# A positive part moved to VectorE, a square to ScalarE, and one sum over four corners in place of two

## What is computed

```python
# mixer, x normalised over channels
t = einsum('bhwc,cd->bhwd', x, W).reshape(B, hw, C)
xn = xf * rsqrt(max(sum(xf * xf, -1), EPS))
sim = power(relu(einsum('bic,bjc->bij', xn, xn)), 2.0)
y = einsum('bij,bjc->bic', sim, t)
...
# deformable convolution: each of nine taps is read at a position of its own
value = (hh * hw * v1 + hh * lw * v2 + lh * hw * v3 + lh * lw * v4) * mask[..., None]
out = einsum('nhwc,cf->nhwf', value, w)
```

## Time and profile before

| | before |
|---|---|
| median of 3 runs (lowest, highest) | 4405.45 us (4403.4, 4419.57) |
| profiled execution | 4427.31 us |
| its span, first to last instruction | 4425.5 us |
| busy PE / PEld | 66% / 43% |
| busy DVE / ACT / POOL | 55% / 40% / 66% |
| mean granted TensorE clock | 0.704 |

### The profile page before, as it was taken

One profiled execution on the slowest core, in us unless ns is written; L12 is line 12 of the kernel. 1 busy time (PEld: TensorE's weight loads), 2 busy tenths in 40 slices (PEclk: granted clock), 3 DMA queues, 4 the chain that ended last, 5 costly groups with the idle time before them and its releaser, 6 DMA issues.

```text
span 4425.5 us, 51603 instructions
## 1 busy us (share of the span) xinstructions
PE 2910.2 (66%) x17810; PEld 1891.5 (43%) x17810; DVE 2435.6 (55%) x3747; ACT 1761.2 (40%) x2959; POOL 2925.6 (66%) x2608
## 2 busy tenths in 40 slices
PE   5969687586757786777777676788681357146432
PEld 2434534452446345633465345633460146135321
DVE  6354454744675456655665466655654245345775
ACT  5656466245523562355425552365231112122210
POOL 0040074777777776777767777777777777776770
PEclk8979798678856895678667886589665556555555
DMA  5000214321533132423342144313351325243446
GB/s 123 8 15 9 39 24 102 100 77 50 127 96 96 39 106 82 131 54 97 85 116 77 51 110 111 110 33 107 87 133 47 104 88 131 62 127 91 121 111 120
DMA packets 540746, 375.76 MB, mean 85 GB/s; under 512 B 465872, under 2 KB 470736, under 8 KB 540496
## 3 DMA queue, kind: packets, MB, share of 16 engines
q0 software_dynamic: 110848, 257.07, 20.1%
q1 hardware_dynamic: 429648, 115.40, 12.5%
HBM read 308.79 MB, written 89.41 MB: 90 GB/s over the span
## 4 chain that ended last, share of the span: by engine, by line
POOL 43%; PE 23%; issue 13%; DVE 11%; ACT 4%; DMA 3%; DVEq 2%; SPq 1%; ACTq 0%; POOLq 0%
POOL G L548 28%; PE PS L1689 22%; POOL shared L562 9%; POOL slot_rows L554 6%; DVE G L623 2%; DMA G<-corner_table,index 2%; DVE G L629 1%; DMA out<-experts_w 1%; DVEq L625 1%; DVE small L972 1%; DVE value L631 1%; PE PS L1724 1%; DVE st L590 1%; ACT small L1551 0%; DVE smallc L590 0%
## 5 line engine op out<-in xcount | busy, mean ns | idle before, releaser
L548 POOL DMA_INDIRECT G<-corner_table,index x1800 | 2029.3, 1127 | 681.6 <-issue 537.0
L623 DVE TENSOR_TENSOR G<-G,corner_w 128x768 f32<-128x768 f32 x600 | 541.5, 953 | 678.2 <-DMA G<-corner_table,index 678.1
L1515 ACT ACTIVATE work<-PS 128x768 f32<-128x768 f32 (+2 forms) x800 | 643.2, 822 | 541.9 <-PE PS L1689 277.8
L1689 PE MATMUL PS<-xn 128*128 128x400 f16 (+3 forms) x3200 | 647.9, 346 | 236.0 <-ACT work L1515 229.8
L951 DVE TENSOR_TENSOR work<-work 128x768 f32<-128x768 f32 (+2 forms) x496 | 479.7, 973 | 457.0 <-PE PS L1689 415.3
L554 POOL DMA_INDIRECT slot_rows<-split_a,slot x400 | 485.1, 1213 | 335.1 <-DVE slot L1046 213.5
L562 POOL DMA_INDIRECT shared<-slot_results,slot x400 | 410.1, 1025 | 349.5 <-DMA slot_results<-shared 227.8
L1689 PE MATMUL PS<-work,xm 128*64 128x400 f32 (+3 forms) x3200 | 638.0, 517 | 0.0
L1689 PEld LDWEIGHTS PS<-xn 128*128 128x128 f16 (+1 forms) x3200 | 289.8, 101 | 666.4 <-ACT work L1515 389.2
L1724 PE MATMUL PS<-ident,value 128*128 128x128 f32 x800 | 181.8, 370 | 522.3 <-DVE xq L636 275.5
L1423 ACT ACTIVATE val_cm<-PS 128x512 f32<-128x512 f32 x200 | 119.1, 596 | 694.5 <-PE PS L1724 694.3
(11 more groups left out here) (266 smaller groups left out, 3591.7 us busy)
## 6 DMA issues: line engine op xcount, KB each, us to landing
G<-corner_table,index POOLq DMA_INDIRECT x1800
corner_table<-rows_scratch SPq DMA_DIRECT2D x32, 784.0 KB
shared<-slot_rows SPq DMA_DIRECT2D x32, 512.0 KB, 7.6
slot_results<-shared SPq DMA_DIRECT2D x32, 512.0 KB
corner_table<-G SPq DMA_DIRECT2D x8, 841.0 KB, 10.5
slot_rows<-split_a,slot POOLq DMA_INDIRECT x400
shared<-slot_results,slot POOLq DMA_INDIRECT x400
experts_w<-x_scratch SPq DMA_DIRECT2D x8, 784.0 KB, 6.2
```

The source lines that it names most:

```text
L548: GP.indirect_dma_start(G[0:rows, n % 2, tap * 4 * C:(tap + 1) * 4 * C], None, tables[b % 2], bass.IndirectOffsetOnAxis(ap=index[0:rows, c ...
L623: V.tensor_tensor(g, g, bc(w, 2, C), ALU.mult)
L1515: A.activation(relu[0:rows, u % 2, :, 0:n], PS[u % 2][0:rows, :, 0:n], ACT.Relu).then_inc(s["relu_done"], 1)
L1689: return P.matmul(o, a, b, start=start, stop=stop, skip_group_check=True)
```

## The change

Five of eight steps swap engines: in steps 1, 2, 4, 5 and 7 VectorE takes the positive part straight from PSUM and ScalarE squares, so that ScalarE now squares in all eight steps and takes the positive part in 0, 3 and 6. TensorE's next similarities wait for either engine's positive part; both wait on one counter of squares, `squared`. In the weighing, the two sums become one `tensor_reduce` over the corner axis, whose input is read with channels ahead of corners; there are four pieces instead of five, and the last of them stands at step 6 of a body and waits for `val_tr`.

```diff
-MIX_SAMPLE, MIX_EVAC, MIX_ADD, MIX_WEIGH = (0, 2, 4, 6), (1, 3, 5), 7, (2, 3, 4, 6, 7)
+MIX_SAMPLE, MIX_EVAC, MIX_ADD, MIX_WEIGH = (0, 2, 4, 6), (1, 3, 5), 7, (2, 3, 4, 6)
...
                     dve.drain()
-                    if piece == 4 and b * T + t > 0:
+                    if piece == 3 and b * T + t > 0:
                         dve.wait_ge(s["val_tr"], 2 * (b * T + t))
                     if piece == 3:
-                        V.tensor_tensor(g[:, :, 0:2, :], g[:, :, 0:2, :], g[:, :, 2:4, :], ALU.add)
-                    else:
-                        V.tensor_tensor(value[:, :].rearrange("p (n c) -> p n c", n=TAPS), g[:, :, 0, :], g[:, :, 1, :],
-                                        ALU.add).then_inc(s["valued"], 1)
+                        red(value[:, :].rearrange("p (n c) -> p n c", n=TAPS), g.rearrange("p n s c -> p n c s")).then_inc(s["valued"], 1)
...
                             if u in DVE_STEPS:
-                                dve.wait_ge(s["relu_done"], g + u + 1)
-                                free = squares_taken(hn, g + u)
-                                if free > 0:
-                                    dve.wait_ge(s["mixed"], free)
-                                V.tensor_tensor(sq[0:rows, u % 4, :, 0:n], relu[0:rows, u % 2, :, 0:n], relu[0:rows, u % 2, :, 0:n],
-                                                ALU.mult).then_inc(s["sq_dve"], 1)
+                                dve.wait_ge(s["sim_done"], g + u + 1)
+                                if g + u > 1:
+                                    dve.wait_ge(s["squared"], g + u - 1)
+                                V.tensor_scalar(relu[0:rows, u % 2, :, 0:n], PS[u % 2][0:rows, :, 0:n], 0.0, None,
+                                                ALU.max).then_inc(s["relu_dve"], 1)
                             beside_mixer(k, j, u)
...
+            def square_step(s_no, half, jh, u):
+                hn, rows, n = s_no // SPH, tile_rows(jh * JB + u // 2), IWS[half]
                 if u in DVE_STEPS:
-                    act.wait_ge(s["sq_dve"], square_dve(hn, jh, u))
+                    act.wait_ge(s["relu_dve"], relus_dve(hn, jh, u))
                 else:
-                    act.wait_ge(s["sq_act"], square_act(hn, jh, u))
+                    act.wait_ge(s["relu_act"], relus_act(hn, jh, u))
+                free = squares_taken(hn, s_no)
+                if free > 0:
+                    act.wait_ge(s["mixed"], free)
+                A.activation(sq[0:rows, u % 4, :, 0:n], relu[0:rows, u % 2, :, 0:n], ACT.Square).then_inc(s["squared"], 1)
...
                         for u in range(steps(jh)):
-                            if g + u + 1 < g0 + SPH:
-
+                            if u + 1 in ACT_STEPS and u + 1 < steps(jh):
                                 if u:
-                                    squared(hn, jh, u - 1)
-                                elif jh:
-                                    squared(hn, jh - 1, SPB - 1)
+                                    act.wait_ge(s["squared"], g + u)
                                 relu_step(g + u + 1, half, jh, u + 1)
-                            if u in ACT_STEPS:
...
+                            if u == SPB - 1:
+                                act.wait_ge(s["squared"], g + u)
+                                relu_step(g + SPB, half, jh + 1, 0)
+                            square_step(g + u, half, jh, u)
                             beside_mixer(k, j, u)
...
                                 if not last:
-                                    pe.wait_ge(s["relu_done"], g + u + 1)
+                                    wait_relu(hn, jh, u)
                                     sims(half, jh * JB + (u + 2) // 2, u)
```

More of the change, by code:

```diff
@@ L218, in metaformer_kernel @@
             f_centered f_squared f_var f_std f_scaled f_cast f_split f_tr f_cm
-            sim_done relu_done sq_act sq_dve mixed z_ready y_done
+            sim_done relu_act relu_dve squared mixed z_ready y_done
             logits_done sm_shift sm_exp hot_ready pos_done slots_ready expert_ready
@@ L289, in steps, with relus_act, relus_dve @@
             return SPB if jh < FULL else 2
-        def square_act(half_no, jh, u):
+        def relus_act(half_no, jh, u):
             return half_no * ACT_H + jh * ACT_N + ACT_STEPS.index(u) + 1
-        def square_dve(half_no, jh, u):
+        def relus_dve(half_no, jh, u):
             return half_no * DVE_H + jh * DVE_N + DVE_STEPS.index(u) + 1
@@ L929, in beside_mixer @@
                     sample_add(k - 3, late_sample(j))
-                for piece in range(5):
+                for piece in range(4):
                     if valid(k - 3) and j in LATE_WEIGH and MIX_WEIGH[piece] == u:
@@ L1514, in relu_step @@
                 act.wait_ge(s["sim_done"], s_no + 1)
-                A.activation(relu[0:rows, u % 2, :, 0:n], PS[u % 2][0:rows, :, 0:n], ACT.Relu).then_inc(s["relu_done"], 1)
-            def squared(hn, jh, u):
+                A.activation(relu[0:rows, u % 2, :, 0:n], PS[u % 2][0:rows, :, 0:n], ACT.Relu).then_inc(s["relu_act"], 1)
+            def square_step(s_no, half, jh, u):
+                hn, rows, n = s_no // SPH, tile_rows(jh * JB + u // 2), IWS[half]
                 if u in DVE_STEPS:
-                    act.wait_ge(s["sq_dve"], square_dve(hn, jh, u))
+                    act.wait_ge(s["relu_dve"], relus_dve(hn, jh, u))
                 else:
-                    act.wait_ge(s["sq_act"], square_act(hn, jh, u))
+                    act.wait_ge(s["relu_act"], relus_act(hn, jh, u))
[3 more added lines that the diff above has]
+                A.activation(sq[0:rows, u % 4, :, 0:n], relu[0:rows, u % 2, :, 0:n], ACT.Square).then_inc(s["squared"], 1)
             def mixer(k):
@@ L1808, in sims, with wait_relu @@
                 ins.then_inc(s["sim_done"], 1)
+            def wait_relu(hn, jh, u):
+                if u in ACT_STEPS:
+                    pe.wait_ge(s["relu_act"], relus_act(hn, jh, u))
+                else:
+                    pe.wait_ge(s["relu_dve"], relus_dve(hn, jh, u))
             def mix(half, hn, jh, u):
@@ L1813, in mix @@
                 rows = tile_rows(j)
[L1814 to L1817, removed]
+                pe.wait_ge(s["squared"], hn * SPH + jh * SPB + u + 1)
                 for b in range(2):
@@ L1865, in mixer @@
                     if not half:
-                        pe.wait_ge(s["relu_done"], g0 + SPH)
+                        wait_relu(hn, FULL, 0)
+                        wait_relu(hn, FULL, 1)
                         sims(1, 0, 0)
```

6 lines of the change are left out of this document (removed).

## The result

The changed kernel took 4439.64 us (median of 4 executions, 4435.14 to 4444.32) against 4404.42 for the kernel before in the same comparison: ratio 1.0073, 95% interval 1.0052 to 1.0094. A second comparison, with 11 executions against 22, gave 1.0044 (1.0026 to 1.0062). It is slower, by 19 us (the second ratio) to 35 us (the medians of the first comparison), where the prediction said 70.

What follows compares the result with a forecast made beforehand. From 550 us until the last gathers the prediction took POOL's transfers plus its waits for `value` as the bound. 4427 + 61 + 7 = 4495 us, brought to the runs' median 21.9 us lower, gave 4475 us, range 4265 to 4565.

Steps and rivals of the forecast that it cites:

- I take 4.7 us: VectorE's one sum over corners: 4.7 us, from writes 16 bytes apart, with 2.56 and 5.5 us as ends.
- x: How much later each tile's `value` is: 4.7 + 0.08 (gap) - 2.20, about 2.5 us, 200 times.
- +61: Tile-by-tile total over images 0 to 7, later `value` set against freed transfers: 61 us slower.
- the 7 us of the moved wait: Wait for TensorE's reading of the last `value`, now ahead of the whole sum: +7 us, from five places totalling 12.6 us.
- the second rival: In between: one sum of 3.6 to 4.2 us, kernel 4374 to 4431 us, mostly within 0.5%; chance 0.08.
- So the mixer's pace stays TensorE's, and I cost this at nothing: Engine swap in the mixer: ScalarE needs 9.2 us per eight-step body, TensorE 11.4, so cost 0.
- a sign of being wrong: The prediction is wrong if the first mixers change by more than a few us; 68 us expected for the first half.
- from the sixth slice ... never under 6 tenths: POOL's busy share in 110.6 us slices: never under 6 tenths from the sixth (553 us) to the thirty-eighth.
- The squares' 75 us: 165 POOL transfers ending 0.82 us after a VectorE square (L951), 0.46 us longer each: 75 us freed, as part of a ceiling.
- In image 7 ... 21 tiles x 2.5 = +52: Image 7: VectorE also works on the selection and never catches up, so 21 tiles pay 2.5 us each: +52 us.
- The first (2.56 us): First rival: the sum runs at the pace of elements in a row; 4289 us, 2.6% faster; chance 0.32.
- That POOL would be freed of nothing: Third rival: POOL's transfers stay held up or run into the next product; 4569 us; chance 0.05.

Runs made afterwards that it cites:

- second profile of before: The kernel before, unchanged, run and profiled again against itself: 4417.12 us against 4415.63, ratio 0.9986; its profiled execution took 4420.0 us.

## Why the prediction was off

**What held.** The bound, and what frees it: POOL's transfers lost 204 us of busy time (190 were counted, as a ceiling; the other 14 were not taken apart), gathers take 1047 ns (1050 was said), no transfer of over 1.0 us ends 0.82 us after a positive part, POOL's wait for `value` passed 250 us. VectorE's positive part (954 ns) and the lower bound of the sum (2.56 us, measured 2.553 over neighbours) came out to 1%. ScalarE's busy time rose by 25 us, where some 16 were worked out.

**The step that failed** is "I take 4.7 us" for the one sum. It measured 4.11. The value was taken from VectorE's writes with a step of 16 bytes, and this read with a step of 256 costs less: beyond the fit's fixed 0.15 us it is 1.72 ns an element, where the fit to those writes gave 1.93 and the neighbours' read takes 1.04. Why a read costs less than a write was not tested. By the prediction's own reckoning 4.11 us makes x 1.99 us in place of 2.58, and the sum +14 in place of +61; with the 7 us of the moved wait that is 21 us over before, within the measured 19 to 35. The duration lies in the second rival's range (3.6 to 4.2 us), which had a chance of 0.08. (The prediction's points do not quite agree here: it puts +19 on a sum of 4.2 us and on one of 4.3; a line from its 4.2 to its 4.7 us gives +27 at 4.3, so its range of slower times should begin near 4440.) Read against the Trainium skill, "Advanced Engine Details and Errata", section "Memory Cachelines": that a new line for each element makes an access slower is borne out for reads too, 4.11 against 2.55 us.

**What the sum hid.** That 21 agrees so well is partly luck. The runs of the parts show three terms off, which partly cancel, and a fourth that no run isolates:

- "So the mixer's pace stays TensorE's, and I cost this at nothing" holds in units 0 and 1 to a percent or so and not in unit 2. From the first product with squares to the last, the halves of units 0 and 1 take 67.2, 69.6, 67.6 and 69.6 us (66.6, 69.1, 66.6 and 69.1 in the second profile of before), those of unit 2 with the swap alone 89.8 and 87.6 (86.1 and 82.7). Unit 2's two halves with the gap between them take 187 to 189 us in all five profiles with the swap in it, and 178 to 179 in the seven without. That is 10 of the 12 us by which the first gather starts later on average (728 to 733 us against 716 to 721). It is what the prediction gave as a sign of being wrong, first mixers that change by more than a few us. Of the 10 us, 5.5 are longer waits of TensorE for positive parts (25.8 against 20.3). The other 4.4 are a longer busy time of TensorE (161.4 against 157.1), some of it at a lower clock: in the swap alone the granted clock was 0.50, 1.2 GHz, in the 4.6 us behind the wait of 4.5 us, and in the second profile of before it was 1.00 from 700 us to the end of the unit. The earlier trace rows has the place: "from the sixth slice ... never under 6 tenths" overlooks the seventh slice (664 to 774 us), which shows 4, since POOL waits there for unit 2's indices; a third mixer, not two, stands ahead of the gathers. In the first half of the changed kernel the chain still shows TensorE, in two pieces where the earlier trace rows has one of 68.08 us:

```profile
59.50 63.12 PE PS L1683 x352
...
122.64 4.88 PE PS L1683 x27
```

  What was not asked is who is behind whom: the positive part frees a bank of PSUM for TensorE, and on VectorE it stands behind layer norms, offsets and experts' results, some of which wait for others.
- The squares' 75 us were to be worth 55. They are worth 22 (the run with the swap from unit 3 on). The reckoning let VectorE keep up wherever it had waited for a gather; but tiles 17 to 22 are weighed in the bodies of the mixer and the `value` of tile 23 stands 18 to 19 us behind its last product (16 to 18 before), however early the gather is done, and POOL spends the gain at tile 0:

```profile
1209.83 4.06 DVE L590 TENSOR_REDUCE value<-G 128x576 f32<-128x2304 f32 x1 [0.79 <-PE PS L1683]
...
1214.66 0.96 POOL L548 DMA_INDIRECT G<-corner_table,index  x1 [14.97 <-DVE value L590]
```

  In the second profile of before that wait was 4.9 us here and 0.3 to 0.8 at the next four images; in the changed kernel it is 15 to 16 us at each of the five, 77 in all.
- "In image 7 ... 21 tiles x 2.5 = +52" was too much even with 1.99 (+42). Image 7 grew by 25 us, measured from the last `value` of image 6. Some of the longer sum falls into waits that were there: in eleven tiles VectorE asks TensorE for a count, and in four of them that wait was 2.5 to 3.0 us. In the second profile of before, and the changed kernel, at the same tile:

```profile
4144.69 0.76 DVE L631 TENSOR_TENSOR value<-G 128x576 f32<-128x576 f32 x1
...
4152.09 0.21 DVE L1239 TENSOR_TENSOR got<-PS,kf 112x49 f32<-112x49 f32 x1 [2.54 <-PE PS L1689]
```

```profile
4144.12 4.10 DVE L590 TENSOR_REDUCE value<-G 128x576 f32<-128x2304 f32 x1
...
4153.48 0.21 DVE L1235 TENSOR_TENSOR got<-PS,kf 112x49 f32<-112x49 f32 x1 [1.50 <-PE PS L1683]
```

  The wait falls from 2.54 to 1.50 us, all eleven from 21.8 to 16.5, and the waits for gathers of the first six tiles from 11.7 to 5.0. Over the whole of image 7 VectorE is busy 48 us more (257 to 305) and idle 23.5 us less (132.3 to 108.8), which is the 25: about half of the longer sums falls into idle time.
- "One wait moves too ... +7" took the five places where TensorE was late before. Ahead of the one sum VectorE waits for TensorE at 46 tiles, 84.7 us in all, and 80.9 us in the kernel with the one sum alone; none of it is in image 7. How much of these 72 us more is on the path is open: no run has the one sum without this wait.

**The rivals.** The first (2.56 us) needed another layout; with it the kernel is 72 us faster, not 124 less 7. Its trace shows the first two losses above; whether they are the whole difference was not measured. That POOL would be freed of nothing is out.

One reading behind these rivals is too wide: that no transfer that begins inside an operation with one operand in PSUM takes over 1.0 us. In the trace of before five do (1.53 to 1.64 us). They bear out its rule all the same: the next operation, which has both operands in SBUF, begins 0.35 to 0.38 us into the transfer, and four of the five end 0.82 us after it (the fifth 0.90):

```profile
1765.50 0.68 DVE L1069 TENSOR_TENSOR yw<-PS,fb2r 112x512 f32<-112x512 f32 x1
1765.72 1.56 POOL L548 DMA_INDIRECT G<-corner_table,index  x1 [15.53 <-DVE value L631]
...
1766.10 0.35 DVE L792 TENSOR_TENSOR small<-om,grid 128x198 f32<-128x198 f32 x1
```

## What to carry to other kernels

Before an operation that gives a buffer back to another engine is moved into another stream, ask who waits for it and what stands ahead of it there: behind long or waiting work it holds that engine up (here 12 to 16 us ahead of the first gather), and the move pays only where what it frees is worth more (22 us where units 3 to 7 alone have it). A slower form of an operation that spares the bounding engine is worth having only where that engine sets the pace: at 103 chosen tiles of 200 the same sum made this kernel 1.3% faster, at all 200 it made it 0.4% slower. And time the parts of a change one by one before trusting a reckoning that comes near the right total.

## What the runs showed that was not expected

A VectorE reduction whose neighbours in the sum lie 256 bytes apart takes 1.61 times as long as one over neighbours (4108 against 2553 ns for the same 2304 elements). While one runs, POOL's indirect transfers take the 0.95 us that they take undisturbed, as they did beside the shorter reductions of the earlier trace rows; in image 7 of the changed kernel:

```profile
4158.22 4.05 DVE L590 TENSOR_REDUCE value<-G 128x576 f32<-128x2304 f32 x1
4159.27 0.95 POOL L548 DMA_INDIRECT G<-corner_table,index  x1 [0.30 <-issue]
4160.52 0.95 POOL L548 DMA_INDIRECT G<-corner_table,index  x1 [0.30 <-issue]
4161.77 0.95 POOL L548 DMA_INDIRECT G<-corner_table,index  x1 [0.30 <-issue]
```
